# Target loop of a two-layer graph network: one float product a step in place of two, products laid out by pair of edges, ranks in two halves, transposes in pairs

## The chip, the cores and the metric

The kernel runs on one core of a Trainium2 chip. The metric is the time of one launch in microseconds of device time. TensorE (PE), VectorE (DVE), ScalarE (ACT), GpSimd (POOL) and the queue of SyncE (SP) run their own programs and meet at semaphores.

## The reference

A graph has 6,250 nodes with 128 features and 200,000 edges, sorted by target. The first layer makes a hidden row for each edge and normalizes it over all edges:

```python
row, col = (edge_index[0], edge_index[1])
ef = jnp.concatenate([x[row], x[col], edge_attr], axis=-1)
h = ef @ W1 + b1
mu = jnp.mean(h, axis=0)
var = jnp.mean((h - mu) ** 2, axis=0)
h = (h - mu) * jax.lax.rsqrt(var + BN_EPS) * gamma + beta
h = jax.nn.relu(h)
msgs = h @ W2 + b2
sums = jax.ops.segment_sum(msgs, row, num_segments=n_nodes)
counts = jax.ops.segment_sum(jnp.ones((msgs.shape[0],), dtype=msgs.dtype), row, num_segments=n_nodes)
out = sums / (counts + 1.0)[:, None]
return out + x
```

Then a layer norm, three graph convolutions with symmetric degree norms, and a second layer norm. For the change only `var` matters: with p = x @ W1[0:128] + b1 for the source and q = x @ W1[128:256] for the target, the sum of h squared over the edges holds, for every target node, (in-degree) x q squared, 2 x q x (sum of p over its edges), and q times the sums of the edge attributes.

## The kernel before

The nodes lie in 49 blocks of 128. Phase one sorts the edges and builds what the others need: a dense 6,272 x 6,272 matrix A of edge counts (`at_dram`), for every target block the cells of edges by source block (`lrow_dram`, `arow_dram`), and the sums for the batch statistics (`pM`, `pS`). Phase two makes the hidden rows and their sums per source, phase three the convolutions with A. If an edge doesn't fit its cell, a slow general path (`general_path`) does all instead.

The change is in phase one's target loop, `drive(engine, step)`: steps s = 0 to 52, of which 6 to 47 are a hardware loop with two steps a turn and the others are written out. It is a pipeline over target blocks, with the flags `bkt` (block s: bucket its edges), `h_` (block s-1: slot one-hots, cells transposed and stored), `a_` (block s-2: neighbour matrix), `y_` (block s-3: y) and `st_` (block s-4: moments). Each engine has a `step` of its own and the order within it is the order of the code.

A block is read as 34 columns of 128 edges (`rec`, ten fields). VectorE makes `key` (the source block of each edge, zero when it isn't of this target block), `hot_p` (one-hot over 49 source blocks, stored as 17 pairs: `[g, k, u]`, u the odd or even column) and eight `product`s of `hot_p` with the fields (L1138, line of the helper). An edge's rank in its cell is its number among the earlier edges of the same source block. It comes from two parts, put side by side in `sel`: a base (L888: 34 matmuls with `upper` over `hot_p`, counting over the partitions, into 49 columns of `pbk`, copied by ScalarE to `base_2` at L981 and multiplied in at L1159) and the keys of the earlier columns in the same partition (`known`, made by 17 + 1 ScalarE copies at L977 to L979, compared at L1154). L1162 to L1169 add up `sel` to `rank`, and L1111 makes its one-hot `orank`. Then L911 places the edges: 34 matmuls of `orank` (stationary) with the eight products (moving, 8 x 49 = 392 columns) into `pbk`; ScalarE takes that out as `cells` (L1012 to L1014). `slot_hots` (L1111 again) makes the one-hots `hs`, `hd` of source slot and target slot in two halves.

TensorE's `step` runs, in this order: `moments`, the base matmuls, eight transposes of `cells` (L896, one a field), 13 groups of neighbour matmuls (L837 with L841, L842: A, and the counts and attribute sums of sources in `pS` and targets in `pX`), each followed by 12 matmuls of y, the sum of p over the sources of each target (L850, into `pY`), then the products L911. `moments` has two float products: `pM[0:7]` from the seven target sums `t7` with q and q squared (L872), `pM[:, 0:128]` from y and q (L875). ScalarE copies y (`yk`, L998), the seven sums (L1002), the in-degree (L1003), and squares q (L1005), which SP loads (L763, after the moments that used the buffer before). GpSimd adds the diagonal (L788). SP stores the transposed cells in 4 transfers (L767, L769) and the A block (L773).

Behind the loop, VectorE turns `pM` into `cross` and three rows `x_q` (L1187 to L1192) and counts the placed edges (L1194); phase two adds these with matmuls into `st`.

```python
for f in range(8):
    last = nc.tensor.transpose(ptr[0:B, f * P:(f + 1) * P], cells[1 - par][:, f, 0:B], identb[:])
prod = prod_raw[:].rearrange("p (f g k u) -> p f g k u", f=8, g=TG, u=2)
last = nc.tensor.matmul(pbk[:, 0:8 * B], orank[:, i // 2, :, i % 2], prod[:, :, i // 2, :, i % 2], start=i == 0, stop=i == TPB - 1)
```

## Time and profile before

| What | Value |
|---|---|
| median of 3 runs | 3862.35 us (3860.61 to 3865.84) |
| profiled execution | 3861.77 us, span 3859.9 us |
| busy PE (matmul) | 3669.5 us, 95% |
| busy VectorE | 2539.7 us, 66% |
| busy ScalarE | 1509.6 us, 39% |
| busy GpSimd | 960.5 us, 25% |
| L911, product matmuls | 1666, busy 322.2 us |
| L1138, products on VectorE | 392, busy 375.7 us |
| L1111, one-hots on VectorE | 196 of 128x3584 and others, busy 355.2 us and more |

The span is profiler time of one execution, less than its run time by the launch. Busy times of matmuls overlap, since the next starts before the one ahead has left the array; the start-to-start distance tells what one costs in a row. Names stand as out<-in. The target loop lies in the first third, phase two in the second, phase three in the last, where VectorE is nearly idle.

### The profile page before, as it was taken

Reading aid. Unit: us, or ns where it says so; the run is one execution under the profiler, and the core shown is the slowest. Engines: PE = TensorE matmul, PEld = TensorE weight load, DVE = VectorE, ACT = ScalarE, POOL = GpSimd, SP = SyncE. Lnnn points to the kernel's source line nnn. Section 1 sums busy time; section 2 is a strip of 40 time slices with the busy share of each in tenths; the row PEclk is TensorE's granted clock in tenths of the full one; section 3 lists DMA queues with packets and bytes.
Section 4 is the critical chain, followed back from the end, with each engine's and each line's share of the span. In section 5 each row is a group of like instructions: output and inputs, shape, how many; then the busy total and the mean of one; then the engine's idle time right before and its main releaser. Section 6 shows DMA issues by size and latency. Waiting matters only on the chain.

```text
span 3859.9 us, 102290 instructions
## 1 busy us (share of the span) xinstructions
PE 3669.5 (95%) x40133; PEld 2581.9 (67%) x40354; DVE 2539.7 (66%) x3609; ACT 1509.6 (39%) x3772; POOL 960.5 (25%) x890
## 2 busy tenths in 40 slices
PE   4699999999999799999999999997999999999999
PEld 3488888888887577777777777774444444454444
DVE  6899999999995599898989898973111111111112
ACT  5355455545554366666666566663000000000000
POOL 0000000000000377676777677720000000000000
PEclk8799999999999899999999999998999999999999
DMA  7122232232224655555555555544666566656664
GB/s 239 53 88 83 94 91 86 83 98 87 86 83 163 104 156 154 163 159 151 159 157 157 149 158 158 157 148 134 199 196 195 194 195 199 198 190 206 207 208 134
DMA packets 433687, 571.30 MB, mean 148 GB/s; under 512 B 198688, under 2 KB 358313, under 8 KB 426569
## 3 DMA queue, kind: packets, MB, share of 16 engines
q1 hardware_dynamic: 401768, 510.29, 43.1%
q0 software_dynamic: 25088, 51.43, 4.9%
q10 hardware_dynamic: 6624, 6.42, 0.5%
q8 instruction: 180, 2.95, 0.3%
q14 instruction: 27, 0.21, 0.0%
HBM read 458.48 MB, written 109.53 MB: 147 GB/s over the span
## 4 chain that ended last, share of the span: by engine, by line
PE 91%; DVE 4%; SPq 2%; issue 1%; ACT 1%; DMA 1%; ACTq 0%; DVEq 0%
PE py L1641 30%; PE ph L1345 10%; PE pY L850 10%; PE pSum L1362 10%; PE pbk L911 8%; PE ph L1348 7%; PE pA L837 4%; PE ph L1340 3%; PE pX L842 2%; PE pS L841 1%; PE pbk L888 1%; PE ptr L896 1%; DVE prod_raw L1138 1%; PE pg L1629 1%; PE ph L1323 1%
## 5 line engine op out<-in xcount | busy, mean ns | idle before, releaser
L1294 POOL DMA_INDIRECT q<-pq_dram,chosen x784 | 861.6, 1099 | 397.5 <-issue 201.9
L1641 PE MATMUL py<-ring_raw,p 128*128 128x512 bf16 (+1 forms) x3822 | 784.6, 367 | 18.0 <-DVE dummy L1801 16.1
L1345 PE MATMUL ph<-p,prod_raw 128*128 (+1 forms) x7056 | 684.1, 219 | 19.8 <-DVE prod_raw L1488 12.2
L1641 PEld LDWEIGHTS py<-ring_raw,p 128*128 128x128 bf16 x3822 | 362.4, 98 | 431.8 <-DVE dummy L1801 16.5
L1345 PEld LDWEIGHTS ph<-p,prod_raw 128*128 128x128 bf16 x7056 | 493.4, 98 | 120.7 <-issue 2.6
L1405 ACT ACTIVATE x<-ph 128x512 bf16<-128x512 f32 x588 | 351.8, 598 | 463.2 <-PE ph L1348 335.9
L1348 PE MATMUL ph<-q,prod_raw 128*128 128x128 bf16 x4704 | 521.2, 220 | 0.0
L1362 PE MATMUL pSum<-x,ring_raw 128*128 128x384 bf16 x2401 | 500.4, 328 | 8.0 <-DVE x L1506 7.9
L850 PE MATMUL pY<-p,ring_raw 128*128 128x128 bf16 x7203 | 500.4, 219 | 0.4 <-issue 0.4
L1501 DVE SCALAR_TENSOR_TENSOR ring_raw<-ph,x 128x512 f32<-128x512 f32 x588 | 404.7, 688 | 128.8 <-ACT x L1405 128.8
L1817 DVE TENSOR_TENSOR yt<-py,dinv_row 128x512 f32<-128x512 f32 (+1 forms) x39 | 25.8, 661 | 696.5 <-PE py L1641 696.5
L970 ACT ACTIVATE ring_raw<-pA 128x512 bf16<-128x512 f32 (+1 forms) x637 | 358.3, 572 | 249.4 <-PE pA L837 246.9
L1694 ACT ACTIVATE hT<-yt,cb 128x512 f32<-128x512 f32 (+1 forms) x39 | 27.2, 697 | 1036.4 <-DVE yt L1817 1036.4
L1506 DVE TENSOR_TENSOR x<-ring_raw,x 128x512 bf16<-128x512 f32 (+1 forms) x637 | 416.4, 654 | 0.1
L850 PEld LDWEIGHTS pY<-p,ring_raw 128*128 128x128 bf16 x7203 | 408.8, 97 | 0.6 <-issue 0.6
L1641 PE MATMUL py<-ring_raw,g 128*128 128x512 bf16 (+1 forms) x1911 | 391.1, 367 | 1.9 <-DVE dummy L1829 1.9
L1392 ACT ACTIVATE x<-ring_raw 128x512 bf16<-128x512 f32 (+1 forms) x637 | 382.7, 601 | 15.9 <-DVE ring_raw L1501 9.3
L1138 DVE TENSOR_TENSOR prod_raw<-q 128x1666 bf16<-128x1666 bf16 x392 | 375.7, 1022 | 15.2 <-PE pbk L911 14.0
L788 POOL TENSOR_TENSOR ring_raw<-ring_raw,identb 128x128 bf16 (+1 forms) x49 | 80.5, 1643 | 1167.9 <-ACT ring_raw L970 1167.9
L1111 DVE TENSOR_TENSOR ring_raw<-iota_lo,x 128x3584 bf16<-128x3584 bf16 x196 | 355.2, 1873 | 13.0 <-PE pX L842 13.0
L911 PE MATMUL pbk<-prod_raw,q 128*128 128x392 bf16 x1666 | 322.2, 351 | 27.7 <-DVE q L1111 27.7
L1348 PEld LDWEIGHTS ph<-q,prod_raw 128*128 128x128 bf16 x4704 | 330.6, 98 | 0.0
(329 smaller groups left out, 4293.1 us busy)
## 6 DMA issues: line engine op xcount, KB each, us to landing
ring_raw<-at_dram SPq DMA_DIRECT2D x252, 896.0 KB, 4.8
at_dram<-ring_raw SPq DMA_DIRECT2D x49, 1568.0 KB, 5.6
prod_raw<-lrow_dram SPq DMA_DIRECT2D x147, 384.0 KB
prod_raw<-lrow_dram SPq DMA_DIRECT2D x196, 256.0 KB
prod_raw<-lrow_dram SPq DMA_DIRECT2D x49, 416.0 KB
q<-pq_dram,chosen POOLq DMA_INDIRECT x784
arow_dram<-x SPq DMA_DIRECT2D x147, 73.5 KB
x<-arow_dram SPq DMA_DIRECT2D x147, 54.0 KB
```

Of the source, the lines that this page charges most:

```text
L850: last = nc.tensor.matmul(pY[:, 0:D], abuf[1 - par][:, b, :], p3[:, b, m3, :], start=b == m3 == 0, stop=b == B - 1 and m3 == 2)
L911: last = nc.tensor.matmul(pbk[:, 0:8 * B], orank[:, i // 2, :, i % 2], prod[:, :, i // 2, :, i % 2], start=i == 0, stop=i == TPB - 1)
L970: nc.scalar.activation(abuf[u][:, 4 * g:4 * g + w, :], pA[(g + u) % 2][:, 0:w * P].rearrange("p (b d) -> p b d", d=P), ACT.Copy).then_inc( ...
L1138: return V.tensor_tensor(prod[:, f, :, :, :], hot_p, rec[u][:, 2 + f, :].rearrange("p (g u) -> p g u", u=2).unsqueeze(2).to_broadcast(dims ...
L1294: nc.gpsimd.indirect_dma_start(q_rows[i][:, k, :], None, pq_rows, bass.IndirectOffsetOnAxis(ap=chosen[u][:, i, k:k + 1], axis=0)).then_inc ...
L1345: last = nc.tensor.matmul(bank[:, k * P:(k + 1) * P], T[q][:, 0, at:at + P], p_b[:, :, m3, :].rearrange("p a d -> p (a d)"), start=False, ...
L1348: last = nc.tensor.matmul(bank[:, k * P:(k + 1) * P], T[q][:, 1, to_q:to_q + P], q3[:, c, m3, :], start=False, stop=m3 == 2 and k == w - 1)
L1362: last = nc.tensor.matmul(pSum[u][:, 0:3 * D], hotf[q][:, at // 2, :, at % 2], zb[which(g)][:, k, :, :].rearrange("p m d -> p (m d)"), sta ...
L1392: nc.scalar.activation(zb[which(g)][:, 0:w, 1, :], res[which(g)][:, 0:w, :], ACT.Copy).then_inc(S["z_mid"], 1)
L1501: V.scalar_tensor_tensor(out=res[u][:, 0:w, :], in0=hidden, scalar=0.0, in1=zb[u][:, 0:w, 0, :], op0=ALU.max, op1=ALU.subtract).then_inc(S ...
L1506: V.tensor_tensor(zb[u][:, 0:w, 2, :], res[u][:, 0:w, :], zb[u][:, 0:w, 1, :], ALU.subtract).then_inc(S["z_low"], 1)
L1641: last = nc.tensor.matmul(py[par][:, 0:w], g3[c % 2][:, 7 * i + m, k, :], ring[i][:, 0:w // P, m, :], start=i == m == k == 0, stop=i == m ...
```

## The change

One: the moments. ScalarE's square of q becomes a copy of q scaled by the in-degree (L1005); the copy of y is dropped, and VectorE makes, at the end of its own step, `ym[:, 0:128]` = 2 y + degree x q from `pY` and that copy. The seven sums lie in the same tile, and one product q x `ym` of 135 columns gives all of `pM` that was two. Behind the loop the 7 columns are copied, turned by a TensorE matmul with the identity and multiplied into two rows of `x_q`. Two: `prod` is laid out with the pair g outermost, so that the 392 moving elements of a matmul are in one run with a constant step. Three: the 34 columns are ranked as two halves of 18 and 16. A second set of 49 base columns is made (all of the first half with `onesb`, the second with `upper`), `known` and its comparison shrink to the two triangles, and `sel` from 83 to 67 columns. Four: transposes of two fields at once, with the pad column, so that `rows_t` holds a field of each pair in partitions 0 to 48 and 50 to 98; SP stores each half by itself.

```diff
+HALF = 9
-SEL = B + TPB
+SEL = B + 2 * HALF
-                prod = prod_raw[:].rearrange("p (f g k u) -> p f g k u", f=8, g=TG, u=2)
+                prod = prod_raw[:].rearrange("p (g f k u) -> p g f k u", f=8, g=TG, u=2)
...
-                                put(sp, S["m_used"], s - 2)
+                                put(sp, S["m_used"], s - 3)
...
-                            sp.dma_start(lrow_dram[:, :, one, :].rearrange("b f c s -> b f (c s)"), rows_t[1 - par][0:B, 0:2, :]).then_inc(rows_out[1 - par], 16)
-                            for j in range(3):
-                                sp.dma_start(arow_dram[:, 6 * j:6 * j + 6, one, :].rearrange("b f c s -> b f (c s)"), rows_t[1 - par][0:B, 2:8, :]).then_inc(rows_out[1 - par], 16)
+                            for h in range(2):
+                                own = rows_t[1 - par][BW * h:BW * h + B]
+                                sp.dma_start(lrow_dram[:, h:h + 1, one, :].rearrange("b f c s -> b f (c s)"), own[:, 0:1, :]).then_inc(rows_out[1 - par], 16)
+                                for k in range(3):
+                                    sp.dma_start(arow_dram[:, 6 * k + h:6 * k + 6:2, one, :].rearrange("b f c s -> b f (c s)"), own[:, 1:4, :]).then_inc(rows_out[1 - par], 16)
...
-                        if y_:
-                            pe.wait_ge(S["q_squared"], s - 2)
-                            last = nc.tensor.matmul(pM[0:7, D:3 * D], t7[1 - par][:], qp[1 - par].rearrange("p a d -> p (a d)"), start=False, stop=False)
                         if st_:
                             pe.wait_ge(S["y_kept"], s - 3)
-                            last = nc.tensor.matmul(pM[:, 0:D], yk[par], qp[par][:, 0, :], start=False, stop=False)
+                            last = nc.tensor.matmul(pM[:, 0:D + 7], qp[par][:, 0, :], ym[par], start=False, stop=False)
...
-                                last = nc.tensor.matmul(pbk[:, BASE:BASE + B], upper[:], hot_p[:, i // 2, :, i % 2], start=i == 0, stop=i == TPB - 1)
+                                later, hot = i >= 2 * HALF, hot_p[:, i // 2, :, i % 2]
+                                if not later:
+                                    nc.tensor.matmul(pbk[:, BASE:BASE + B], upper[:], hot, start=i == 0, stop=False)
+                                last = nc.tensor.matmul(pbk[:, BASE + B:BASE + 2 * B], upper[:] if later else onesb[:], hot, start=False, stop=i == TPB - 1)
...
-                            for f in range(8):
-                                last = nc.tensor.transpose(ptr[0:B, f * P:(f + 1) * P], cells[1 - par][:, f, 0:B], identb[:])
+                            for j in range(4):
+                                last = nc.tensor.transpose(ptr[0:2 * BW, j * P:(j + 1) * P], cells[1 - par][:, 2 * j:2 * j + 2, :].rearrange("p f b -> p (f b)"), identb[:])
...
-                                last = nc.tensor.matmul(pbk[:, 0:8 * B], orank[:, i // 2, :, i % 2], prod[:, :, i // 2, :, i % 2], start=i == 0, stop=i == TPB - 1)
+                                last = nc.tensor.matmul(pbk[:, 0:8 * B], orank[:, i // 2, :, i % 2], prod[:, i // 2, :, :, i % 2].rearrange("p f k -> p (f k)"), start=i == 0, stop=i == TPB - 1)
...
-                        if y_:
-                            act.wait_ge(S["y_ready"], s - 2)
-                            nc.scalar.activation(yk[1 - par], pY[:, 0:D], ACT.Copy).then_inc(S["y_kept"], 1)
...
-                            nc.scalar.activation(t7[par][:], pX[:, 0:7], ACT.Copy)
+                            nc.scalar.activation(ym[par][:, D:D + 7], pX[:, 0:7], ACT.Copy)
...
-                            nc.scalar.activation(qp[par][:, 1, :], qp[par][:, 0, :], ACT.Square).then_inc(S["q_squared"], 1)
+                            nc.scalar.activation(qp[par][:, 1, :], qp[par][:, 0, :], ACT.Copy, scale=ym[par][:, D + 6:D + 7]).then_inc(S["q_squared"], 1)
...
-                            first = mark(V.tensor_tensor(sel[:, :, 0:41, :], sel[:, :, 0:41, :], sel[:, :, 42:83, :], ALU.add))
+                            first = mark(V.tensor_tensor(sel[:, :, 0:33, :], sel[:, :, 0:33, :], sel[:, :, 34:67, :], ALU.add))
...
+                        if y_:
+                            dve.wait_ge(S["y_ready"], s - 2)
+                            dve.wait_ge(S["q_squared"], s - 2)
+                            V.scalar_tensor_tensor(out=ym[1 - par][:, 0:D], in0=pY[:, 0:D], scalar=2.0, in1=qp[1 - par][:, 1, :], op0=ALU.mult, op1=ALU.add).then_inc(S["y_kept"], 1)
```

TensorE around the start of a looped step (pM are the moments, `pbk<-q` the bases from `hot_p`, ptr the transposes), before:

```order
L911 MATMUL pbk<-prod_raw,q 128x392 x34
L630 REGISTER_ALU
L630 COMPARE_AND_BRANCH
L872 MATMUL pM<-x,t 7x256
L875 MATMUL pM<-x 128x128
L888 MATMUL pbk<-q,upper 128x49 x34
L896 MATMUL ptr<-identb,x 49x128 x8
L837 MATMUL pA<-ring_raw 128x128 x4
```

and now (the pair of L891 and L892 comes 18 times in all):

```order
L915 MATMUL pbk<-prod_raw,q 128x392 x34
L631 REGISTER_ALU
L631 COMPARE_AND_BRANCH
L876 MATMUL pM<-x 128x135
L891 MATMUL pbk<-q,upper 128x49
L892 MATMUL pbk<-q,onesb 128x49
```

```order
L892 MATMUL pbk<-q,upper 128x49 x16
L900 MATMUL ptr<-identb,x 100x128 x4
L841 MATMUL pA<-ring_raw 128x128 x4
```

One matmul of the moments is left, and between it and the neighbours stand 52 matmuls and 4 transposes in place of 34 and 8.

VectorE from the last written-out step with new edges (48) through step 49 to the end of the loop (3584 and 2816 are the slot one-hots), before:

```order
L1111 TENSOR_TENSOR q<-iota_lo,rank 128x4352
L1111 TENSOR_TENSOR ring_raw<-iota_lo,x 128x3584 x2
L1111 TENSOR_TENSOR ring_raw<-iota_lo,x 128x2816 x2
L1111 TENSOR_TENSOR ring_raw<-iota_lo,x 128x3584 x2
L1111 TENSOR_TENSOR ring_raw<-iota_lo,x 128x2816 x2
L1185 TENSOR_SCALAR deg_all<-in_degree 128x49
```

and now:

```order
L1118 TENSOR_TENSOR q<-iota_lo,rank 128x4352
L1118 TENSOR_TENSOR ring_raw<-iota_lo,x 128x3584 x2
L1118 TENSOR_TENSOR ring_raw<-iota_lo,x 128x2816 x2
L1188 SCALAR_TENSOR_TENSOR x<-pY,x 128x128
L1118 TENSOR_TENSOR ring_raw<-iota_lo,x 128x3584 x2
L1118 TENSOR_TENSOR ring_raw<-iota_lo,x 128x2816 x2
L1188 SCALAR_TENSOR_TENSOR x<-pY,x 128x128 x3
L1198 TENSOR_SCALAR deg_all<-in_degree 128x49
```

The read of `pY`, which was ScalarE's, stands behind the slot one-hots of its step, and TensorE's moments of the next step wait for it.

TensorE from the end of step 49 into step 50, where there are neither products nor bases, before:

```order
L850 MATMUL pY<-p,ring_raw 128x128 x3
L872 MATMUL pM<-x,t 7x256
L875 MATMUL pM<-x 128x128
L837 MATMUL pA<-ring_raw 128x128 x4
L841 MATMUL pS<-x,ring_raw 128x7
```

and now:

```order
L854 MATMUL pY<-p,ring_raw 128x128 x3
L876 MATMUL pM<-x 128x135
L841 MATMUL pA<-ring_raw 128x128 x4
L845 MATMUL pS<-x,ring_raw 128x7
L846 MATMUL pX<-x,ring_raw 128x7
```

The matmul of step 50 that read the q times of step 49's block (L872) is gone; what is left waits for the fused y of the block before.

## Rows read from the trace of the kernel before

**Rows 1.** One stretch: busy us (instructions) of PE, PEld, DVE, ACT, POOL; clock; DMA.

```profile
250.00:1150.00 900.00, 895.34 (x14835) 738.51 (x14833) 885.71 (x836) 465.54 (x1596) 66.90 (x40) 1.00 0.29 89
```

**Rows 2.** Waits from 200 to 1350 us: us in total, times, longest.

```profile
ACT x L1012 <- PE pbk L911: 261.8, 45, 5.9
...
DVE prod_raw L1138 <- PE pbk L911: 5.4, 21, 0.3
```

**Rows 3.** Chain of waits, a looped step: start us, us, what.

```profile
703.67 6.30 PE pbk L911 x34
710.42 0.56 ACT x L1014
...
713.26 0.68 PE pY L850 x12
713.95 0.23 PE pA L837 x4
...
726.42 6.29 PE pbk L911 x34
732.71 0.53 PE pM L872 x2
733.24 0.42 PE pM L875 x2
```

**Rows 4.** Lines (ns min/median/max, first and last start); chain pieces of later stages.

```profile
L911 PE MATMUL pbk<-prod_raw,q x34: 344/346/350, 726.3 to 732.4; 128*128 128x392 bf16 x34
L888 PE MATMUL pbk<-q,upper x34: 183/186/192, 711.1 to 712.0; 128*128 128x49 bf16 x34
L896 PE MATMUL ptr<-identb,x x8: 219/219/238, 712.1 to 712.5; 128*49 128x128 bf16 x8
L911 PE MATMUL pbk<-prod_raw,q x1564: 344/346/350, 182.9 to 1207.9; 128*128 128x392 bf16 x196
...
2000.95 0.66 PE pSum L1362 x4
...
3016.57 0.89 PE pg L1629 x8
3017.46 2.59 PE py L1641 x12
```

**Rows 5.** Timeline of VectorE through a step: start us, us, line, operation.

```profile
708.71 0.24 DVE L1143 SCALAR_TENSOR_TENSOR key<-q,iota_c 128x34 bf16<-128x34 bf16 x1
710.07 3.84 DVE L1138 TENSOR_TENSOR prod_raw<-q 128x1666 bf16<-128x1666 bf16 x4
...
718.23 1.02 DVE L1159 TENSOR_TENSOR q<-q,base 128x1666 bf16<-128x1666 bf16 x1
...
721.73 2.43 DVE L1111 TENSOR_TENSOR q<-iota_lo,rank 128x4352 bf16<-128x4352 bf16 x1
...
731.25 0.24 DVE L1143 SCALAR_TENSOR_TENSOR key<-q,iota_c 128x34 bf16<-128x34 bf16 x1
```

**Rows 6.** Timeline of VectorE behind the loop.

```profile
1259.50 0.29 DVE L1188 TENSOR_TENSOR x<-pM,x 128x128 f32<-128x128 f32 x1
```

**Rows 7.** Timeline of SP's queue, a looped step and step 49.

```profile
715.39 1.39 SPq L769 DMA_DIRECT2D arow_dram<-x  x3
...
1222.99 0.39 SPq L763 DMA_DIRECT2D x<-pq_dram  x1
```

**Rows 8.** Timelines behind step 49, and a stretch (busy, clock 0.50).

```profile
1232.14 1.02 PE L872 MATMUL pM<-x,t 128*7 128x256 f32 x2 [8.04 <-ACT x L1005]
...
1236.63 0.33 PE L837 MATMUL pA<-ring_raw 128*128 128x128 bf16 x3
...
1231.77 0.31 ACT L1005 ACTIVATE x<-x 128x128 f32<-128x128 f32 x1 [7.23 <-DMA x<-pq_dram]
...
1224.03 3.39 DVE L1111 TENSOR_TENSOR ring_raw<-iota_lo,x 128x2816 bf16<-128x2816 bf16 x2 [2.98 <-PE pX L842]
...
1229.00:1235.00 6.00, 2.86 (x23) 1.95 (x24) 0.00 (x0) 0.88 (x2) 0.00 (x0) 0.50 0.78 281
```

71 lines of the change are left out of this document (40 added, 31 removed).

## Prediction, before the changed kernel was run

> A measurement of this kernel can tell from no change about 0.2%, some 7.7 us. The profiled execution took 3861.77 us with a span of 3859.9 us, 0.6 us under the median of 3862.35 us, so a sum made against the one serves for the other.
>
> **What bounds the kernel now.** I looked first at the busy time by stage. In 900 us of the target loop TensorE is busy for 895 and VectorE for 886, while ScalarE has 466 and GpSimd 67 [rows 1]: two engines are nearly full, so a saving on one is worth only what the other leaves. The waits tell which is ahead: ScalarE spends 262 us waiting for the product matmuls (45 times, 5.8 us each); VectorE waits 5.4 us for the same matmuls, 21 times, so it arrives just ahead of them [rows 2]. Then the chain of waits through a step: product matmuls start at 703.67 and at 726.42, and all but about 1.2 us between is PE [rows 3]. From the products of step 3 to those of step 48 there are 45 steps: 1,564 = 46 x 34 matmuls start from 182.9 to 1207.9, less the 6.1 us of the last burst 1018.9 us, **22.64 us** each [rows 4]. VectorE from key to key takes 22.54 us (708.71 to 731.25), and goes from one operation straight to the next [rows 5]; its 5.4 us of waits, spread over 45 steps, leave it some 22.52 us of its own [rows 2]. So TensorE sets the end, by 0.12 us a step.
>
> **TensorE's step.** The base counts grow from 34 matmuls of 49 columns to 52 (18 upper, 18 onesb, 16 upper). Now 34 start from 711.1 to 712.0 [rows 4], 33 intervals in 0.9 us, 27 ns each: +18 x 27 = **+0.49 us**. All on the path.
>
> The transposes go from 8 with 49 columns to 4 with 100 columns of stationary data (two fields and their pad). Eight take 0.4 us for 7 intervals, 57 ns each, 0.46 us in all [rows 4]. The wider weight load isn't shown; the bounds are 57 ns as now and 111 ns, the fp32 matmul with a stationary of 128 columns (0.89 us for 8) [rows 4], so the four cost 0.23 to 0.44 us. I take the middle, 84 ns, as 100 columns lie between the two: **-0.12 us**, with ends of -0.23 and -0.02.
> The Trainium skill (TensorE: Matmul & The Clock Gate, section on LDWEIGHTS) gives a weight load as its columns over 1.2 GHz, 83 ns for 100; by it the term would be -0.13 us. No run here shows it.
>
> The product matmuls are the core. 34 of 392 columns start from 726.3 to 732.4: 33 intervals in 6.1 us, 185 ns each. But 384 columns take 165 ns (0.66 for 4), 512 columns 216 ns (2.59 for 12) [rows 4], 0.4 ns a column, from which 392 columns should take 168 ns. What differs is how the moving operand lies: today it is 8 pieces (one a field) of 49 elements 4 bytes apart, 3,332 bytes from piece to piece; now it becomes one piece of 392 elements 4 bytes apart. Neither piece nor step is dear alone: the 512-column matmul reads 4 pieces of 128 contiguous elements and is at the line's 216 ns, and the neighbour matmuls L837, 128 elements 4 bytes apart in one piece, take 58 ns against 57 for L850's contiguous ones [rows 3]. So the 17 ns come with short, odd pieces (49 elements, 196 bytes), which vanish. Bounds: 185 ns (nothing gained) and 166 ns (nothing left over the 384-column row). I take 168: 34 x 17 = **-0.58 us**.
> The Trainium skill (Advanced Engine Details and Errata, section Memory Cachelines) wants at least two hits on a 16-byte line. A piece of 196 bytes ends in a line with a single hit, and the merged operand has none; by it the sum would be the same, but no run here shows it.
>
> The fp32 moments go from two matmuls, 0.53 + 0.42 us [rows 3], to one of 135 columns (some 0.44). I cost this at **nothing** in the loop: it runs while PE waits for ScalarE to empty the product bank (cells L1014 ends at 710.98, base matmuls start at 711.1) [rows 3, 4]. Without it the gap stays, since L1012 to L1014 are unchanged. If that cover were gone it would be worth 0.5 us. In the other step of a pair the chain passes the moments themselves [rows 3], at most 0.1 us may be won.
>
> Together: 22.64 + 0.49 - 0.12 - 0.58 = **22.43 us**, -0.21 a step.
>
> **VectorE's step.** From 1666 to 4352 elements an operation grows from 1.02 to 2.43 us [rows 5], 0.52 ns an element; four products in a row take 3.84 us, so one more instruction in a queue costs 0.94 - 0.87 = 0.07 us. The comparison with the known keys: 1156 to 324 + 256 elements, -0.30 + 0.07. The multiply by the bases is split in two: +0.07. The three adds lose 476 elements: -0.25; the reduction, 374 to 306 at 1.04 ns: -0.07. New is the fused y, 128 fp32 elements from PSUM: 0.29 us in an operation of that size from PSUM [rows 6], less overlap: +0.25. The products write 17 pieces of 98 instead of one of 1666; L1159 does that already and takes 1.02 us as they do [rows 5]: nothing. Sum -0.23: **22.3 us**, below TensorE's 22.43. TensorE stays the bound, by the same 0.13 us.
>
> **Others.** ScalarE drops the y copy, its transposed copy is 512 elements wide, not 1024, and it gains one small copy of keys and 98 columns of base; it waits 5.8 us a step, nothing. SP issues 8 row transfers a step instead of 4: 4 x 0.46 us (1.39 for 3) [rows 7], done at 716.8, and its next work, the A block, isn't there before ScalarE's last evacuation, near the next products at 726.4 [rows 3]: nothing.
>
> Waits added: VectorE's fused y waits for y (end of the neighbour matmuls, just ahead of the products at 703.67) and for q times degree (ScalarE's next work behind those), but stands behind slot one-hots that run up to the key at 708.71 [rows 5], so both have come. Behind it stands the next key, only as late as its own 0.25 us. PE's moments now wait for it: at 708.7 + 0.3 = 709.0, and the products ahead of them on PE end at 710. No stall in the loop.
>
> **Sum.** Loop: 45 x -0.21 = **-9.5 us**. Before it, the first three steps have little neighbour work and, as an estimate from the terms above, follow VectorE, without a fused y: 3 x -0.4 = **-1.2 us**.
>
> **Tail.** Step 50 has no products to hide anything. Today PE ends step 49 at 1224.1 and stands 8.04 us for ScalarE's square, which waits 7.23 us for q (issued by SP only at 1222.99, behind the reload of q3); the third group of neighbours starts at 1236.63 [rows 7, 8]. Now PE waits there for the fused y only. That stands behind two one-hots that VectorE can start only when PE ends step 49 (1224.03, 3.39 us): 1227.4 + 0.3 + 0.6 for the moments, so the neighbours start at 1228.3. Two groups fill both banks; ScalarE is still waiting for q until 1232.08, empties the first bank by 1232.7, and the third group starts at 1232.8, not 1236.63: 3.8 us, of which I keep 3.0, since PE would still stand still, in two pieces, and today's stand leaves a granted clock of 0.50, the level of 1.2 GHz, from 1229 to 1235 [rows 8], which may come again, for a group or two. Shorter moments in step 51 (-0.3) and two links fewer at 0.33 us before the count, less a wait (-0.4) [rows 6]: tail **-3.7 us**.
>
> Total -9.5 - 1.2 - 3.7 = -14.4: 3861.8 - 14.4 = 3847.4, on the medians **3848 us**.
>
> **Rivals.**
> *The products stay at 185 ns* (slower). If the 17 ns belong to 4-byte steps over a long run, merging does nothing: PE's step is 22.64 + 0.49 - 0.12 = 23.01, the loop +16.6, with -4.9 elsewhere +11.7 us: **3874 us**. Against it is L837 with its 4-byte step; for it, that no row shows such a step beyond 128 columns. Each ns of the product interval is 34 x 45 = 1.5 us; from 177 ns on the change loses, from 182 ns by over 0.2%.
> *A limit on bytes.* L837 moves 512 bytes of span in 57.5 ns, 8.9 a ns. Were that a limit, 392 elements would need 176 ns, -0.31 us: step 22.70, +2.7 in the loop, -4.9 outside: **3860 us**, no change. For it: 185 ns is 8.5 a ns; against it, nothing says L837 is at a limit.
> *VectorE becomes the bound.* If 17 pieces cost 0.03 us a product and the fused y 0.5 with its two waits, its step is 22.79: +6.8, -4.9, **3864 us**. For it: only 0.13 us of room; against it, L1159.
> *The tail gives nothing* (q lands later still, or the stall is paid elsewhere): +3.7 on the forecast, 3852 us, still faster; inside the range.
> *The change doesn't do what it says* would be a rank that is wrong and sends the run down the general path, far longer: I give it nothing.
>
> **How the numbers follow.** Forecast 0.66, with its own range from 3839 (VectorE's 22.3 as the floor, the full tail) to 3854. Products at 185 ns 0.13, the byte limit 0.13, VectorE 0.08. Faster by over 0.2% is the forecast with a little of the byte limit, 0.67; within 0.2% 0.20; slower 0.13. The range runs from 3839 to 3866: it holds the forecast, the byte limit and VectorE's case, and leaves out most of the 185 ns case.
>
> **What would show it.** Right: product starts 168 ns apart, 22.4 us from one step's products to the next, VectorE's wait before its first product about as long as now, the gap between products and base unchanged at 1.2 us though the moments have halved, the third group of step 50 some 4 us nearer to the end of step 49. Wrong: products still near 185 ns; VectorE without any wait and PE waiting for hot_p or ranks; base matmuls over 27 ns with alternating weights; a PE stall ahead of the moments in the loop.

## The result, and the profile after

The changed kernel takes **3836.34 us** (median of 4 runs, 3835.38 to 3838.11), the kernel before 3861.93 us (4 runs, 3860.61 to 3865.84) on the same chip: a ratio of 0.9932, 95% interval 0.992 to 0.9944, 25.6 us less. The forecast was 3848 us with a range from 3839 to 3866: the direction was right, the gain almost twice as large as forecast, and the time lies below the range. The profiled execution took 3838.11 us with a span of 3836.3 us, 23.6 us under the span before; the sums below are made against the spans.

The stretch of [rows 1], the columns as there:

```profile
250.00:1150.00 900.00, 867.64 (x15618) 755.88 (x15616) 890.32 (x974) 458.82 (x1628) 79.87 (x40) 1.00 0.30 92
```

TensorE has lost its fullness, 868 of 900 us in place of 895, and VectorE has gone from 886 to 890. The waits in the same stretch (us in total, times, longest), to be read against [rows 2], which go from 200 to 1350 us:

```profile
ACT x L1018 <- PE pbk L915: 216.6, 41, 5.3
PEld pbk L891 <- DVE q L1154: 20.3, 21, 1.0
PE pbk L891 <- DVE q L1154: 19.7, 25, 0.8
PE pbk L891 <- ACT x L1020: 12.7, 16, 0.8
```

VectorE's wait for the product matmuls, 5.4 us before, is gone from the list. In its place TensorE waits ahead of the base matmuls for VectorE's `hot_p` (L1154) in 25 steps and for ScalarE's cells (L1020) in 16: the two end within some 0.02 us of each other, around 1.21 us behind the start of the last product. The page's chain says the same. Before, it was PE 91% and DVE 4%; now (shares of the span by engine, then by line):

```profile
PE 65%; DVE 24%; issue 8%; SPq 2%; ACT 1%; DMA 1%; DVEq 0%; ACTq 0%
PE py L1654 30%; PE ph L1358 11%; PE pSum L1375 10%; DVE prod_raw L1145 8%; PE ph L1361 7%; DVE ring_raw L1118 6%; PE ph L1353 3%; DVE q L1154 1%; DVE q L1171 1%; DVE q L1167 1%; PE pY L854 1%; DVE q L1168 1%; DVE rank L1178 1%; DVE q L1173 1%; PE pbk L915 1%
```

So VectorE now carries the chain through the target loop, with its products (L1145) and one-hots (L1118). Its timeline through one step, in place of [rows 5]:

```profile
719.57 0.28 DVE L1188 SCALAR_TENSOR_TENSOR x<-pY,x 128x128 f32<-128x128 f32 x1
719.77 0.24 DVE L1150 SCALAR_TENSOR_TENSOR key<-q,iota_c 128x34 bf16<-128x34 bf16 x1
720.04 1.03 DVE L1154 TENSOR_TENSOR q<-iota_blk,key 128x1666 bf16<-128x1666 bf16 x1
721.10 3.83 DVE L1145 TENSOR_TENSOR prod_raw<-q 128x1666 bf16<-128x1666 bf16 x4
724.86 0.32 DVE L1161 TENSOR_TENSOR q<-x,key 128x324 bf16<-128x324 bf16 x1
725.10 0.29 DVE L1162 TENSOR_TENSOR q<-x,key 128x256 bf16<-128x256 bf16 x1
725.30 3.83 DVE L1145 TENSOR_TENSOR prod_raw<-q 128x1666 bf16<-128x1666 bf16 x4
729.04 0.62 DVE L1167 TENSOR_TENSOR q<-q,base 128x882 bf16<-128x882 bf16 x1
...
732.28 2.42 DVE L1118 TENSOR_TENSOR q<-iota_lo,rank 128x4352 bf16<-128x4352 bf16 x1
734.63 7.25 DVE L1118 TENSOR_TENSOR ring_raw<-iota_lo,x 128x3584 bf16<-128x3584 bf16 x4
741.81 0.28 DVE L1188 SCALAR_TENSOR_TENSOR x<-pY,x 128x128 f32<-128x128 f32 x1
742.01 0.24 DVE L1150 SCALAR_TENSOR_TENSOR key<-q,iota_c 128x34 bf16<-128x34 bf16 x1
```

There is no bracket, so no idle time, in the whole step, which is 22.24 us long from key to key (719.77 to 742.01). And TensorE's lines in one step (ns min/median/max, first and last start), to be held against [rows 4]:

```profile
L915 PE MATMUL pbk<-prod_raw,q x34: 332/334/338, 714.1 to 719.9; 128*128 128x392 bf16 x34
L900 PE MATMUL ptr<-identb,x x4: 219/220/238, 722.6 to 722.7; 128*100 128x128 bf16 x4
L915 PE MATMUL pbk<-prod_raw,q x1564: 332/334/338, 180.6 to 1186.9; 128*128 128x392 bf16 x196
```

46 bursts of 34 products start from 180.6 to 1186.9; less the 5.72 us of the last burst, 45 steps take 1000.5 us, **22.23 us** each against 22.64.

Where the 23.6 us went, from the starts of the product bursts and the ends of the stages, in both traces:

| Stretch | before | after | difference | forecast |
|---|---|---|---|---|
| to the products of step 3 | 182.88 | 180.63 | -2.25 | -1.2 |
| steps 3 to 48 (45 steps) | 1018.91 | 1000.52 | -18.4 | -9.5 |
| from step 48's products to the test, at the end of phase one, that every edge fits (`fits`) | 60.11 | 55.75 | -4.36 | -3.7 |
| the rest | | | +1.4 | 0 |

### The profile page after: what moved, and what is told of

It reads as the page before. It is cut to its first block, busy times and chain, and to the rows that moved or that the text cites. A ratio compares the mean times of both kernels' runs of the same rounds, so it can differ in the third digit from the quotient of the medians.

```text
span 3836.3 us, 104225 instructions
## 1 busy us (share of the span) xinstructions
PE 3620.9 (94%) x40721; PEld 2589.0 (67%) x40942; DVE 2525.0 (66%) x3757; ACT 1489.2 (39%) x3772; POOL 967.4 (25%) x890
## 4 chain that ended last, share of the span: by engine, by line
PE 65%; DVE 24%; issue 8%; SPq 2%; ACT 1%; DMA 1%; DVEq 0%; ACTq 0%
PE py L1654 30%; PE ph L1358 11%; PE pSum L1375 10%; DVE prod_raw L1145 8%; PE ph L1361 7%; DVE ring_raw L1118 6%; PE ph L1353 3%; DVE q L1154 1%; DVE q L1171 1%; DVE q L1167 1%; PE pY L854 1%; DVE q L1168 1%; DVE rank L1178 1%; DVE q L1173 1%; PE pbk L915 1%
## 5 line engine op out<-in xcount | busy, mean ns | idle before, releaser
L1308 POOL DMA_INDIRECT q<-pq_dram,chosen x784 | 851.4, 1086 | 405.3 <-ACT ph L1411 204.1
L1145 DVE TENSOR_TENSOR prod_raw<-q 128x1666 bf16<-128x1666 bf16 x392 | 375.6, 1022 | 9.5 <-PE pbk L915 7.8
L792 POOL TENSOR_TENSOR ring_raw<-ring_raw,identb 128x128 bf16 (+1 forms) x49 | 94.1, 1920 | 1130.9 <-ACT ring_raw L976 1130.9
L1118 DVE TENSOR_TENSOR ring_raw<-iota_lo,x 128x3584 bf16<-128x3584 bf16 x196 | 355.2, 1873 | 11.6 <-PE pX L846 11.6
L915 PE MATMUL pbk<-prod_raw,q 128*128 128x392 bf16 x1666 | 302.9, 339 | 25.8 <-DVE q L1118 25.8
```

What stands on the lines that cost most here:

```text
L1118: return V.tensor_tensor(to, iota_lo[:].unsqueeze(1).to_broadcast(dims), of.unsqueeze(2).to_broadcast(dims), ALU.is_equal)
L1145: return V.tensor_tensor(prod[:, :, f, :, :], hot_p, rec[u][:, 2 + f, :].rearrange("p (g u) -> p g u", u=2).unsqueeze(2).to_broadcast(dims ...
L1308: nc.gpsimd.indirect_dma_start(q_rows[i][:, k, :], None, pq_rows, bass.IndirectOffsetOnAxis(ap=chosen[u][:, i, k:k + 1], axis=0)).then_inc ...
```

## The experiments

Fourteen kernels ran. Those with a count of steps in their text are read by the mean step from the products of step 3 to those of step 48, which moves far less than the whole time. Whole times are good to 4 to 6 us, by the intervals of the ratios; the kernel before, measured beside each group of experiments, has medians from 3859.69 to 3861.68 us. Of the longer edits the diffs show a part, cut at `...`.

### Which engine sets the step: what the transposes cost

Theory: TensorE's own step fell by more than forecast, because a change of stationary width costs something (A), and VectorE took over as the bound. The first run undoes the pairs alone: eight transposes of 49 columns and four transfers again.

```diff
-                            for j in range(4):
-                                last = nc.tensor.transpose(ptr[0:2 * BW, j * P:(j + 1) * P], cells[1 - par][:, 2 * j:2 * j + 2, :].rearrange("p f b -> p (f b)"), identb[:])
+                            for f in range(8):
+                                last = nc.tensor.transpose(ptr[0:B, f * P:(f + 1) * P], cells[1 - par][:, f, 0:B], identb[:])
...
```

> The changed kernel with the transposes of before: eight with 49 columns of stationary data in place of four with 100, and SP's four transfers. Theory A (a change of the stationary's width between 128 or 100 and 49 columns costs TensorE some 90 ns each way, beside the 57 ns a transpose): the transposes take 0.41 us more a step, TensorE's step grows from 22.17 to 22.58 us, passes VectorE's 22.24, and the run is 45 x 0.34 = 15 us slower than the changed kernel, some 3851 us; the gaps of 116 ns before the first transpose and 152 ns behind the last come back. Theory B (only the number of transposes counts, 57 ns each): four more are 0.23 us, TensorE's step 22.40, +7 us, some 3843 us.

Measured: 3851.6 us (10 runs), ratio 0.9977 (0.9967 to 0.9986), step 22.62 us. That is theory A (22.58), not 22.40. The second run makes the four wide transposes twice, eight instructions without a change of width:

```diff
-                            for j in range(4):
+                            for j in (0, 0, 1, 1, 2, 2, 3, 3):
```

> The changed kernel with each of its four 100-column transposes done twice, so eight, but no change to a narrow stationary. Theory A: four more at 56 to 60 ns and no gaps of 90 ns: TensorE's step 22.17 + 0.23 = 22.40, against 22.24 now +7 us, some 3843 us. Theory B says the same here and for the eight narrow ones. If a wide transpose in a row costs 83 ns (its weight load), the step is 22.50 and the run some 3848 us.

Measured: 3842.12 us, ratio 0.9949 (0.9932 to 0.9965), step 22.42 us; VectorE waits for the products again (8.7 us in 39 times). Four more transposes made TensorE 0.22 us longer (56 ns each), the step grew by only 0.19: TensorE's own step in the changed kernel is 22.42 - 0.22 = 22.20 us, some 0.04 under VectorE's.

The traces show where the 0.2 us between the two kinds of eight lie. TensorE's timelines at the same place, before and after:

```profile
711.12 1.05 PE L888 MATMUL pbk<-q,upper 128*128 128x49 bf16 x34 [0.21 <-ACT x L1014]
712.10 0.63 PE L896 MATMUL ptr<-identb,x 128*49 128x128 bf16 x8
712.66 0.35 PE L837 MATMUL pA<-ring_raw 128*128 128x128 bf16 x3
```

```profile
722.15 0.58 PE L892 MATMUL pbk<-q,upper 128*128 128x49 bf16 x16
722.56 0.41 PE L900 MATMUL ptr<-identb,x 128*100 128x128 bf16 x4
722.80 0.28 PE L841 MATMUL pA<-ring_raw 128*128 128x128 bf16 x2
```

Before, the eight transposes take 712.10 to 712.66, 0.56 us where seven intervals of 58 ns are 0.41: the first neighbour matmul with its 128 stationary columns starts 152 ns behind the last transpose. At the front the first transpose starts 116 ns behind the last base matmul, now 26. After, the four take 0.24 us, 60 ns each, the way out included.

### Products by layout

The product layout of before, in the changed kernel:

```diff
-                prod = prod_raw[:].rearrange("p (g f k u) -> p g f k u", f=8, g=TG, u=2)
+                prod = prod_raw[:].rearrange("p (f g k u) -> p f g k u", f=8, g=TG, u=2)
...
```

> The changed kernel with the products laid out as before (eight pieces of 49 moving elements). Product matmuls go back from 173 to 185 ns: 34 x 12 = 0.40 us, TensorE's step 22.57, 0.33 over the 22.24 of VectorE: +15 us, some 3851 us, and VectorE waits again before its first product. If the layout cost VectorE something (17 pieces a product), its operations get shorter here than 3.83 us for four; I expect no change.

Measured: 3851.26 us (10 runs), ratio 0.9975 (0.9965 to 0.9984), products 185 ns apart again and a step of 22.60 us. The layout is worth 34 x 11.8 ns = 0.40 us to TensorE, and 22.60 - 0.40 = 22.20 is a second reading of TensorE's own step.

### Access patterns and widths measured by themselves

Bursts of extra matmuls behind the products of step 5, whose results nobody uses. With them the rest of the step is late, so its time says nothing.

```diff
+                                for _ in range(12):
+                                    full(w_s, flat[:, 0:392], 392)
+                                for _ in range(12):
+                                    full(w_s, flat[:, 0:784].rearrange("p (k u) -> p k u", u=2)[:, :, 0], 392)
...
+                                for _ in range(4):
+                                    narrow(64)
+                                for _ in range(4):
+                                    last = wide()
```

> The changed kernel with bursts of 12 extra matmuls into unused columns, in step 5 alone, behind its products; some 30 us longer for that. Start-to-start distances. Moving operand: 392 contiguous 166 ns; 392 at 4-byte steps in one run 173 (as in the kernel); eight pieces of 49 at 4-byte steps 185; eight contiguous pieces of 49: near 185 if the pieces cost it, near 166 if it is the step; eight of 48 at 4-byte steps (384, all on 16-byte lines) 165 to 170 if broken lines cost it, near 182 if the number of pieces does; 384 in one run at 4-byte steps 170. 128 at 4-byte steps 58, contiguous 56. Width of the stationary, by four matmuls each of 128, 49, 128, 64, 128, 65, 128, 100, 128, 7, 128 columns: theory A wants 90 ns more at each change to 49, 64 and 7 columns and back, and none for 65 and 100.

The starts are in the timeline of TensorE; L943 loads 128 columns, L942 the number behind `128*`:

```profile
246.42 0.41 PE L942 MATMUL pX<-prod_raw,identb 128*49 128x128 bf16 x4
246.76 0.40 PE L943 MATMUL pX<-prod_raw,identb 128*128 128x128 bf16 x4
247.09 0.41 PE L942 MATMUL pX<-prod_raw,identb 128*64 128x128 bf16 x4
247.43 0.40 PE L943 MATMUL pX<-prod_raw,identb 128*128 128x128 bf16 x4
247.66 0.39 PE L942 MATMUL pX<-prod_raw,identb 128*65 128x128 bf16 x4
247.89 0.39 PE L943 MATMUL pX<-prod_raw,identb 128*128 128x128 bf16 x4
248.11 0.39 PE L942 MATMUL pX<-prod_raw,identb 128*100 128x128 bf16 x4
248.33 0.39 PE L943 MATMUL pX<-prod_raw,identb 128*128 128x128 bf16 x4
```

Four matmuls of 128 moving columns take 0.23 us (247.66 to 247.89, a stationary of 65; the same for 100 and 128), 0.34 us where the next four have another width on the other side of 64 (246.42 to 246.76 with 49, 247.09 to 247.43 with 64). From the single starts: 56 ns between like ones, 150 ns from 128 to 49, 64 or 7 columns, 152 ns back, and 56 ns from 128 to 65 or 100 and back. So of the widths tried it is the passage between 64 or fewer stationary columns and 65 or more that costs, some 95 ns each way. The second matmul behind a passage is late too in most cases (75 and 80 ns behind the first with 49 and 64 columns, 65 on the way back), which is why four of them lose 0.11 us.

The moving operand, ns from start to start in bursts of twelve:

| Moving operand | ns |
|---|---|
| 392 contiguous | 166 |
| 392 in one run, 4-byte steps (the new layout) | 173.5 |
| 8 x 49 contiguous | 173.4 |
| 8 x 49, 4-byte steps (the old layout) | 183 |
| 384 in one run, 4-byte steps | 169 |
| 8 x 48, 4-byte steps | 171 |
| 128 contiguous / 4-byte steps | 56 / 57.5 |

A 4-byte step costs a run of 392 elements 7.5 ns, and pieces of 49 as much again or a little more (7.4 ns contiguous, 9.5 with the step; the expectation had only 166 or 185 for the contiguous ones); pieces of 48 cost 2 ns. The probe changed two things between 49 and 48, the length of a piece and the distance from one to the next (1666 and 1664 elements), so which of them costs isn't told apart. Whether the stationary is strided makes no difference (173 ns with a contiguous one).

### VectorE's part: the ranks in one piece

Ranks as before (one piece, 34 base matmuls, `sel` of 83 columns) in the changed kernel:

```diff
-SEL = B + 2 * HALF
+SEL = B + TPB
...
-                                if not later:
-                                    nc.tensor.matmul(pbk[:, BASE:BASE + B], upper[:], hot, start=i == 0, stop=False)
-                                last = nc.tensor.matmul(pbk[:, BASE + B:BASE + 2 * B], upper[:] if later else onesb[:], hot, start=False, stop=i == TPB - 1)
+                                last = nc.tensor.matmul(pbk[:, BASE:BASE + B], upper[:], hot_p[:, i // 2, :, i % 2], start=i == 0, stop=i == TPB - 1)
...
```

> The changed kernel with the ranks in one piece again (34 base matmuls, 83 columns of sel). TensorE's step falls by 18 x 26 ns to 21.70 us, VectorE's grows by what its shorter operations gave, about 0.48 us, from 22.24 to 22.72. If VectorE sets the changed kernel's step, as the absent wait before its products says: period 22.72, +0.48 x 45 = +22 us, some 3858 us. If TensorE sets it: 22 to 23 us faster or, with VectorE next, at most unchanged, 3836 us.

Measured: 3857.46 us (10 runs), ratio 0.9994 (0.9985 to 1.0004), step 22.71 us. TensorE has 0.46 us less to do and the kernel is 21 us slower than the changed one: its waits for VectorE fill up, a second one ahead of the moments.

```profile
PEld pM L874 <- DVE x L1178: 38.8, 37, 1.1
PE pbk L887 <- DVE q L1146: 28.3, 37, 0.8
```

The half ranks alone are worth 22.71 - 22.23 = 0.48 us of VectorE's step.

### The float products

Two float products a step as before, y copied by ScalarE, no fused y on VectorE:

```diff
-                            last = nc.tensor.matmul(pM[:, 0:D + 7], qp[par][:, 0, :], ym[par], start=False, stop=False)
+                            last = nc.tensor.matmul(pM[:, 0:D], yk[par], qp[par][:, 0, :], start=False, stop=False)
...
+                            last = nc.tensor.matmul(pM[0:7, D:3 * D], t7[1 - par][:], qp[1 - par].rearrange("p a d -> p (a d)"), start=False, stop=False)
...
```

> The changed kernel with two float products a step, y copied by ScalarE, q squared, as before. VectorE loses the fused y (0.20 us): 22.04. TensorE's gap between products and bases: before it was 1.30 and 1.50 us in turn, the changed one 1.28 at least; if the second wait that ScalarE's queue takes up behind the products in every other step comes back (0.13 us), TensorE's step is 22.29 and sets the period: +0.05 x 45 and +4 us in the tail, some 3842 us. If the moments themselves are in the gap's way, more: 22.4, 3848 us. If neither, 22.17 and 3837 us. The stall of 8 us behind step 49 comes back in any case.

Measured: 3840.62 us (4 runs, 3835.58 to 3846.05), ratio 0.9949 (0.9933 to 0.9966), step 22.26 us against 22.23. VectorE has 0.20 us less, the distance from the fused y to the key (719.57 to 719.77 above), and gives it back in waits for the products (9.8 us in 38 times). ScalarE begins on the cells 0.58 and 0.45 us behind the last product's start in turn, where the changed kernel has 0.45 in every step, and TensorE's bases start 1.49 and 1.27 us behind it. The rest of the 4 us between the two profiled executions is the tail: the last products lie only 0.7 us earlier than the changed kernel's, the fits 4.8 us later (1241.7 against 1236.9). So the fused moments are worth 0.03 us a step to the loop, and the tail's gain belongs to them.

### Loading either engine

An extra operation on VectorE (a clearing of 128x128 floats before the key), and eight extra matmuls of 49 columns behind the bases:

```diff
+                            V.memset(rd, 0.0)
```

> The changed kernel with one more small VectorE operation a step (a memset of 128x128 fp32 into a spare tile, 0.15 to 0.2 us). VectorE sets the step: the period grows by all of it, +7 to +9 us, some 3844 us. Were TensorE the bound with VectorE behind: +4 us or less.

```diff
+                            for _ in range(8):
+                                nc.tensor.matmul(pX[:, 8:8 + B], onesb[:], zerob[:, 0:B], start=True, stop=True)
```

> The changed kernel with eight more 49-column matmuls a step behind the bases (8 x 26 = 0.21 us on TensorE). If TensorE's own step is 22.17 us, 0.07 under VectorE's: period 22.38, +0.14 x 45 = +6.3 us, some 3843 us. If TensorE sets the step already: 22.45, +9.4 us, some 3846 us. If it has more room than I think: less than +5 us.

The first missed: 3833.83 us, 0.9932 (0.9915 to 0.9948), no slower than the change. VectorE's timeline shows why:

```profile
741.04 0.28 DVE L1189 SCALAR_TENSOR_TENSOR x<-pY,x 128x128 f32<-128x128 f32 x1
741.29 0.17 DVE L1148 MEMSET x<- 128x128 f32 x1
741.38 0.13 DVE L1151 SCALAR_TENSOR_TENSOR key<-q,iota_c 128x34 bf16<-128x34 bf16 x1
741.54 1.03 DVE L1155 TENSOR_TENSOR q<-iota_blk,key 128x1666 bf16<-128x1666 bf16 x1
```

The clearing takes 0.17 us but overlaps both its neighbours, and the key's record falls from 0.24 to 0.13 us; why it does, no run shows. From the start of the fused y to that of `hot_p` pass 0.50 us, in the changed kernel 0.47 (719.57 to 720.04): the operation loaded VectorE with 0.03 us only. It was no test.

The second: 3849.29 us (10 runs, 3842.55 to 3852.49), 0.9971 (0.9961 to 0.998), step 22.40 us. 8 x 25 ns on TensorE gave 0.17 us, from which TensorE's own step is 22.20 for the third time. The step says +7.5 us; the median is 13 to 15 us over the change, and the profiled run, at 3842.55, is its fastest. Where the other runs lose 7 us more is not known.

### A test with force on both sides

Since VectorE never pauses, TensorE could be given a whole microsecond of freedom. In t9 the first neighbour group goes ahead of the bases, into the gap behind the products. In t10 the same is done to t6. In t11 VectorE gets an operation whose cost is known beforehand: one of its size (L1162) takes 0.20 us from its start to the next.

```diff
+                        front = both(s, par, 0, a_, y_)
+                        if bkt and y_:
+                            next(front)
                         if bkt:
                             pe.wait_ge(S["hot_ready"], s + 1)
...
```

```diff
+                            V.tensor_tensor(rd.bitcast(BF16).rearrange("p (u d) -> p u d", u=2), identb[:].unsqueeze(1).to_broadcast([P, 2, P]), identb[:].unsqueeze(1).to_broadcast([P, 2, P]), ALU.mult)
                             dve.wait_ge(S["known_ready"], s + 1)
```

> The changed kernel, but TensorE multiplies the first of the thirteen neighbour groups of a step (5 large products, 8 narrow ones and 12 y products, about 1.1 us) between the moments and the base products, where it now stands idle for about 1.0 us; nothing is added or removed, and nothing moves on another engine. If VectorE sets the looped step (22.24 us, without a pause of its own), the loop stays as it is and the kernel takes 3836 (3833 to 3839); VectorE's few waits for the products go. If TensorE were the bound, as the prediction had it, the step would lose about 1.0 us until VectorE stops it at its own length, which by the prediction was 22.3: since the step already takes 22.24, this theory would have to give a gain of at least 0.1 us a step, 3831 or less.

> The kernel of t6 (two float products a step, y copied by ScalarE, so that VectorE's add of y, 0.24 us a step, is gone) with the first neighbour group ahead of the base products as in t9. In t6 VectorE's own step is about 22.24 - 0.24 = 22.0 us, but it waited for the products, and the step took 22.26: the float products fill TensorE's gap and more. If this is right, taking the idle remainder of the gap away lets the step fall to VectorE's 22.0: 45 x 0.26 = 12 us less than t6, about 3829 (3825 to 3833), less than both kernels. If the gap behind the products is not what held t6, it stays at 3841.

> The changed kernel with one more product of 128x256 bf16 numbers on VectorE in each step, behind the first four products of the cells; nobody uses its result. The operation of the same size at L1162 takes 0.20 us from its start to that of the next. If VectorE sets the step, 49 x 0.20 = 10 us more, 3846 (3843 to 3849). If TensorE set it with VectorE 0.13 us shorter, as the prediction had it, 45 x 0.07 = 3 us more, 3839. The clearing of 128x128 float numbers in t7 was no test of this: that operation took the place of a pause inside the next one, which fell from 0.24 to 0.13 us in the timeline.

t9: 3834.07 us, 0.9926 (0.9913 to 0.994), step 22.23 us, equal to the change to a hundredth. The waits ahead of the bases are gone, and TensorE now stands for the fused y, which the moments need, in every step (41 times). The first row has the products' starts, from which the step comes as above:

```profile
L920 PE MATMUL pbk<-prod_raw,q x1564: 332/334/338, 177.8 to 1184.1; 128*128 128x392 bf16 x196
PEld pM L877 <- DVE x L1193: 30.9, 41, 0.8
```

t11: 3843.39 us, 0.9954 (0.994 to 0.9967), step 22.43: +0.20 us, the operation's own, and 7 us between the medians where 45 steps give 9.

```profile
L915 PE MATMUL pbk<-prod_raw,q x1564: 332/334/338, 180.6 to 1195.9; 128*128 128x392 bf16 x196
```

The two agree: **VectorE sets the step.**

t10 missed: 3843.68 us, 0.9957 (0.9944 to 0.9971), step 22.33, not 22.0. VectorE waited for the products still, and TensorE had a wait that t6 has not:

```profile
DVE prod_raw L1153 <- PE pbk L923: 13.1, 40, 0.3
PEld pA L841 <- ACT ring_raw L982: 12.8, 40, 0.3
```

With two float products there was little gap left to fill, and what was gained was given back: the third group finds its bank not yet emptied, 0.3 us a step. ScalarE takes out the group that went ahead (L982, at 703.48) only behind the keys, the bases, for which it waits 0.42 us, and the turned rows; the third group starts at 704.12. The same wait stands in t9 (13.1 us, 41 times), where TensorE had the time for it.

### Taking the fused y off VectorE

Two kernels move the fused y off VectorE without work for TensorE: ScalarE writes 2y, GpSimd adds degree times q. t12 with the group ahead, t13 without.

```diff
-                            V.scalar_tensor_tensor(out=ym[1 - par][:, 0:D], in0=pY[:, 0:D], scalar=2.0, in1=qp[1 - par][:, 1, :], op0=ALU.mult, op1=ALU.add).then_inc(S["y_kept"], 1)
+                            nc.scalar.activation(ym[1 - par][:, 0:D], pY[:, 0:D], ACT.Copy, scale=2.0).then_inc(S["q_squared"], 1)
...
+                            put(pool, S["q_squared"], s * 2 - 4)
+                            nc.gpsimd.tensor_tensor(ym[1 - par][:, 0:D], ym[1 - par][:, 0:D], qp[1 - par][:, 1, :], ALU.add).then_inc(S["y_kept"], 1)
...
```

> The kernel of t9 (first neighbour group ahead of the base products) in which VectorE's add of y is gone: ScalarE writes 2y from PSUM (0.28 us, in a stretch in which it waits anyway), GpSimd adds in-degree times q on it, and TensorE multiplies what it did. So VectorE's step loses 0.24 us and TensorE's nothing is added to, other than in t10, whose float products filled the gap and made TensorE the bound at 22.33. If VectorE set t9's step, this one takes 22.0: 45 x 0.24 = 11 us less, 3824 (3820 to 3828). If GpSimd's add is too late (it has about 5 us), or something else holds 22.24, it stays at 3835 or above.

> The same without the group ahead: VectorE's own step is 22.0, TensorE's own, by the sums of t2, t3 and t8, 22.20. If those sums hold, TensorE sets it at 22.20, 45 x 0.04 = 2 us less than the changed kernel, 3833 (3830 to 3836), and VectorE waits for the products about 0.2 us a step. If VectorE alone set the changed kernel's step and TensorE had room, it is 3825.

Measured: t12 3835.71 us, 0.9931 (0.9917 to 0.9944), step 22.29; t13 3838.57 us, 0.9939 (0.9926 to 0.9953), step 22.29. Both missed; neither is faster than the change by more than the noise. VectorE is still without a pause and the 0.20 us of the fused y are gone, but the slot one-hots, 7.25 us in the changed kernel at 734.63, have grown. VectorE, then GpSimd, in t12:

```profile
735.15 7.52 DVE L1129 TENSOR_TENSOR ring_raw<-iota_lo,x 128x3584 bf16<-128x3584 bf16 x4
```

```profile
714.25 0.90 POOL L792 TENSOR_TENSOR ring_raw<-ring_raw,identb 128x128 bf16 x1 [19.20 <-ACT ring_raw L984]
715.11 2.24 POOL L795 TENSOR_TENSOR x<-x 128x128 f32<-128x128 f32 x1
```

The four one-hots of one step, ns each (two of 3584 elements, then two of 2816), and the one during which an addition of GpSimd starts:

| Kernel | GpSimd starts in | 1st | 2nd | 3rd | 4th |
|---|---|---|---|---|---|
| changed | 2nd (L792) | 2017 | 2018 | 1849 | 1612 |
| t9 | 1st (L792) | 2019 | 2255 | 1612 | 1611 |
| t12 | 1st (L792), 2nd (float) | 2018 | 2254 | 1878 | 1614 |
| t13 | 2nd (L792), 3rd (float) | 2018 | 2017 | 1852 | 1877 |

Rows behind it, t9 and then the third one-hot of t12:

```profile
711.88 0.71 POOL L792 TENSOR_TENSOR ring_raw<-ring_raw,identb 128x128 bf16 x1 [21.53 <-ACT ring_raw L981]
L1123 DVE TENSOR_TENSOR ring_raw<-iota_lo,x x1: 2255/2255/2255, 712.2 to 712.2; 128x3584 bf16<-128x3584 bf16 x1
L1123 DVE TENSOR_TENSOR ring_raw<-iota_lo,x x1: 1612/1612/1612, 714.4 to 714.4; 128x2816 bf16<-128x2816 bf16 x1
```

```profile
L1129 DVE TENSOR_TENSOR ring_raw<-iota_lo,x x1: 1878/1878/1878, 717.0 to 717.0; 128x2816 bf16<-128x2816 bf16 x1
```

The one-hot under way when GpSimd starts isn't touched, and the next one is longer: by 0.24 us behind the bf16 addition of the diagonal, L792 (2255 against 2018, 1849 against 1612), and by 0.26 behind the float addition (1878 and 1877 against 1612). t12 has to be held against t9, in which the second one-hot is the long one already. GpSimd's own time makes no difference: L792 takes 0.71 us in t9 and 1.99 in the changed kernel for the same 0.24. It is so in every kernel here: 47 or 48 of the 196 one-hots are 0.23 to 0.25 us longer than the others of their size, and each of them is the first to start behind a start of L792.

So the 0.20 us saved on VectorE came back as 0.26 us beside GpSimd, and 22.24 - 0.20 + 0.26 = 22.30 is the step of both kernels. And 0.24 us of VectorE's step, before the change and after it, go with the addition of the diagonal on GpSimd. No kernel here runs without that addition, so it isn't shown that VectorE would be faster by as much.

The Trainium skill (SBUF — State Buffer, section SBUF: two separate sides) tells of a port pair that VectorE and GpSimd can only hold in turn, for a whole instruction, the loser blocked. The trace agrees in that the one-hot under way loses nothing and the next one does, but the loss is 0.24 to 0.26 us, not the 0.71 to 2.24 us of GpSimd's additions.

### VectorE's step before the change

The kernel before with the pairs of transposes alone:

```diff
-                            for f in range(8):
-                                last = nc.tensor.transpose(ptr[0:B, f * P:(f + 1) * P], cells[1 - par][:, f, 0:B], identb[:])
+                            for j in range(4):
+                                last = nc.tensor.transpose(ptr[0:2 * BW, j * P:(j + 1) * P], cells[1 - par][:, 2 * j:2 * j + 2, :].rearrange("p f b -> p (f b)"), identb[:])
...
```

> The kernel before with only the transposes made in pairs, four 100 columns wide in place of eight of 49 (and the eight transfers that store them). TensorE's step loses the two changes of width and four transposes, 0.41 us: 22.64 - 0.41 = 22.23, less than VectorE's 22.52, which then sets the step: 45 x 0.12 = 5 us less, 3855 to 3857, and VectorE's waits for the products, 0.12 us a step before, go. If VectorE's step before was shorter than 22.52, the gain shows it: at 22.24 it would be 18 us, 3843.

Measured: 3855.58 us (11 runs), 0.9985 (0.9976 to 0.9994), 6.1 us less than before, step 22.51 us. VectorE's waits for the products are gone and TensorE waits for `hot_p` in 40 steps. So VectorE's step before was 22.51 us, as the prediction read it (22.52).

## Why the prediction was off

**What bounds the kernel before: right.** TensorE at 22.64, VectorE at 22.52; t14 measured 22.51.

**Bases: right.** 52 matmuls at 26 ns with alternating stationaries: +0.46 us where +0.49 was forecast.

**Transposes: the term that failed most**, -0.41 us where -0.12 stood and -0.23 was the outer bound. The interval of 100 columns is near the lower bound, some 60 ns, not the middle at 84. And the sum left out the two changes of width, 90 to 95 ns each, which stand between the last base and the first transpose and between the last transpose and the first neighbour matmul. Both were in the trace before: the last base started at 712.0 and the transposes ran from 712.1 to 712.5 [rows 4], while the neighbours began only at 712.66. The prediction took intervals inside a group and never the way in and out.

**Products: right in kind, too large by 0.18 us.** 173 ns, not 168: -0.40 us against -0.58. The step of 4 bytes costs 7.5 ns in a run of 392, which the neighbour matmul of 128 showed as 1 ns. The 165 ns of the 384-column row was of contiguous operands.

**The gap behind the products: not nothing.** Before, the first base started 1.50 and 1.30 us in turn behind the last product's start, 1.40 in the mean. In t1, t3 and t8, in which TensorE sets the step, it is 1.36 and 1.27, 1.31 in the mean: -0.09 us. (In the changed kernel it is 1.35, since TensorE waits there for `hot_p`.) Before, in every other step, ScalarE began on the cells 0.59 us after the last product's start, not 0.46; now always 0.45. That comes with the moments, since t6, which takes them back, has 0.58 and 0.45 in turn again. I read it so that ScalarE's queue takes up its waits earlier, because the scaled copy of q has a wait more; t6 takes back more than that wait, so the reading isn't shown.

TensorE's step is thus 22.64 + 0.46 - 0.41 - 0.40 - 0.09 = 22.20, as t2, t3 and t8 give it too; forecast 22.43. The transposes fell 0.29 us below their term and the gap 0.09 below its nothing; 0.18 too much on the products hid a good part of that, which was luck.

**VectorE's step: right**, 22.24 for 22.3. The fused y costs 0.20 us where +0.25 stood, the half ranks gave 0.48 (the sum of their terms was -0.48), and four products in a row take 3.83 us as before (3.84), so that the 17 pieces cost nothing.

**The step that failed, then, is "TensorE stays the bound, by the same 0.13 us".** With TensorE 0.23 us too long in the sum, for the passages of stationary width above all, the bound passed to VectorE, which t9 and t11 show, and the loop gave 45 x 0.41 = 18.4 us, not 9.5. The range had VectorE's 22.3 as its floor: 3839 with the full tail. The rest of the miss is VectorE's last 0.06 us (2.8 us) and the start, -2.25 for -1.2. The start was estimated and isn't settled: the products of step 3 began between 177.7 and 181.8 in the fourteen runs.

**Tail: right**, with its mechanism. TensorE stands 3.58 us for the fused y in step 50, not 8.04 for the square, and then 0.93 us for ScalarE ahead of the third group, as forecast. The granted clock is 0.50, the level of 1.2 GHz, from 1205 to 1215 us, behind TensorE's stand from 1202.6 on. The timelines of TensorE and VectorE behind step 49, and a stretch:

```profile
1206.18 0.82 PE L876 MATMUL pM<-x 128*128 128x135 f32 x2 [3.58 <-DVE x L1188]
...
1211.77 0.61 PE L841 MATMUL pA<-ring_raw 128*128 128x128 bf16 x4 [0.93 <-ACT ring_raw L976]
1205.85 0.28 DVE L1188 SCALAR_TENSOR_TENSOR x<-pY,x 128x128 f32<-128x128 f32 x1
1206.00:1212.00 6.00, 4.89 (x53) 4.55 (x54) 0.13 (x1) 1.17 (x3) 0.00 (x0) 0.50 0.76 265
```

**The rivals.** Products at 185 ns and the limit on bytes (176 ns) were wrong: 173 ns in the kernel and in the probe. VectorE as the bound came true, but by TensorE getting shorter, not by VectorE getting longer, and that way wasn't among the rivals: the prediction gave VectorE's case only a price above the forecast. The tail that gives nothing was wrong: without the fused moments (t6) the fits come 4.8 us later.

What the parts are worth at the end: the change needed TensorE and VectorE together. The half ranks are worth 21 us only because pairs and layout made TensorE 0.8 us shorter (t5); the pairs alone give 6 us (t14); each of pairs or layout taken out costs 15 to 17 us (t1, t3).

## What to carry to other kernels

Where two engines are full, work out each one's own step and take the larger; then give each term its error and ask at which sum the bound passes over, since a saving that is underrated on the one makes the other the bound and changes the whole price. Take intervals between unlike instructions too, not only within a group: the cost sat in the passage. A load test must use an operation whose cost in its place is known, and work moved to an idle engine has to be watched for what it does to its neighbour. Where two kernels differ in the order of an engine, as t12 and the changed one do, the comparison goes by the kernel with the same order.

## What was not expected of the hardware

- A matmul with 7, 49 or 64 stationary columns next to one with 128 costs about 95 ns more, in each direction (150 and 152 ns against 56, t4); 65, 100 and 128 columns are alike.
- Moving operands: 392 contiguous elements 166 ns, with 4-byte steps 173.5, in eight pieces of 49 with such steps 183 to 185, in eight of 48 (384 columns) 171 (t4, t3).
- A clearing of 128x128 floats on VectorE between the fused y and the key costs 0.03 us of its 0.17 (t7).
- An addition of 128x128 on GpSimd lengthens the next one-hot that VectorE starts, by 0.24 us if it is bf16 (every kernel; t9 moves it from the third one-hot to the second) and by 0.26 if it is float (t12, t13), however long it takes itself; the one-hot under way stays as it is.
